# Expert stage of a float32 decoder layer: token tiles of 128 slots instead of 112, and the last 48 slots multiplied by two float32 products side by side, for two steps at once

## The reference

```python
logits = xf @ router_w.T; probs = softmax(logits)
topw, topi = top_k(probs, 2);  topw = topw / (topw.sum(-1) + 1e-06)
...                                       # the 560 heaviest tokens of each expert are kept
disp = zeros(E, capacity + 1, D).at[se, pos].set(xf[st])[:, :capacity]
g = einsum('ecd,edf->ecf', disp, wg)
u = einsum('ecd,edf->ecf', disp, wu)
eo = einsum('ecf,efd->ecd', silu(g) * u, wd)
out = zeros_like(xf).at[st].add(gathered_eo * weight)
```

## Time and profile before

| what | value |
|---|---|
| median of 3 runs | 3836.18 us |
| the profiled execution | 3833.68 us |
| its span in the trace | 3831.9 us |
| PE busy | 3662.7 us (96%) |
| PE weight load | 3157.1 us (82%) |
| DVE busy | 2361.7 us (62%) |
| ACT busy | 1737.3 us (45%) |
| POOL busy | 1298.8 us (34%) |
| granted TensorE clock, mean | 0.979 |

### The profile page before, as it was taken

One profiled execution on the slowest core, in us unless ns is written; L12 is line 12 of the kernel. 1 busy time (PEld: TensorE's weight loads), 2 busy tenths in 40 slices (PEclk: granted clock), 3 DMA queues, 4 the chain that ended last, 5 costly groups with the idle time before them and its releaser, 6 DMA issues. The chain is left out here.

```text
span 3831.9 us, 84885 instructions
## 1 busy us (share of the span) xinstructions
PE 3662.7 (96%) x28086; PEld 3157.1 (82%) x28086; DVE 2361.7 (62%) x5526; ACT 1737.3 (45%) x4277; POOL 1298.8 (34%) x1385
## 2 busy tenths in 40 slices
PE   7999999999979999999999999669999999999998
PEld 6888888888768888888888888459989899899987
DVE  6788888888746666666666666665443433434343
ACT  4555555554535555555555555313333333333332
POOL 1333333333325556665656666310101101011010
PEclk9999999999989999999999999779999999999999
DMA  4222222222343444443444443222433424334232
GB/s 125 59 53 62 53 64 54 61 58 59 89 111 97 106 107 111 109 118 101 108 106 107 112 109 100 61 68 79 115 90 107 115 80 119 87 107 119 82 100 62
DMA packets 315533, 347.68 MB, mean 91 GB/s; under 512 B 45247, under 2 KB 231975, under 8 KB 315396
## 3 DMA queue, kind: packets, MB, share of 16 engines
q1 hardware_dynamic: 305796, 318.25, 30.7%
q0 software_dynamic: 9600, 27.58, 2.5%
HBM read 181.62 MB, written 38.65 MB: 57 GB/s over the span
## 5 line engine op out<-in xcount | busy, mean ns | idle before, releaser
L1605 DVE TENSOR_REDUCE x_mx<-x_psS 112x1 f32<-112x752 f32 x512 | 479.6, 937 | 385.8 <-PE x_psS L1158 382.4
L2339 DVE TENSOR_TENSOR hid<-e_psU,act_g 128x280 f32<-128x280 f32 x256 | 115.2, 450 | 684.5 <-PE e_psU L34 662.5
L1440 ACT ACTIVATE x_pt<-x_psE 125x448 f32<-125x448 f32 x768 | 389.5, 542 | 226.9 <-PE x_psE L1170 217.6
L1029 POOL TENSOR_TENSOR part<-x_pt 125x448 f32<-125x448 f32 x255 | 292.4, 1147 | 509.9 <-ACT x_pt L1440 500.9
L1985 POOL DMA_INDIRECT out<-ex_y,sidx x40 | 38.1, 952 | 1046.0 <-DVE ex_y L2372 1036.9
L611 POOL TENSOR_TENSOR qks<-qks,cos 128x448 f32<-128x448 f32 x128 | 148.1, 1157 | 676.2 <-DMA qks<-qk 676.2
L2130 ACT ACTIVATE act_g<-e_psG 128x280 f32<-128x280 f32 x256 | 103.7, 405 | 470.2 <-PE e_psG L34 456.1
L1158 PE MATMUL x_psS<-k_st,q_st 97*112 97x376 f32 x1024 | 287.7, 362 | 22.8 <-DMA k_st<-mk 14.7
L32 PE MATMUL pj<-xT_hi,win_hi 128*128 128x224 f32 x1024 | 302.7, 296 | 1.5 <-DVE xT_lo L651 1.3
L32 PE MATMUL e_psG<-ex_hi,g_hi 128*128 128x280 f32 x1024 | 303.1, 296 | 0.9 <-issue 0.9
L32 PE MATMUL e_psU<-ex_hi,u_hi 128*128 128x280 f32 x1024 | 298.3, 291 | 3.7 <-DVE hid L2339 2.8
(11 more groups left out here) (293 smaller groups left out, 10712.5 us busy)
## 6 DMA issues: line engine op xcount, KB each, us to landing
k_st<-kT SPq DMA_DIRECT2D x768, 93.8 KB, 2.2
raw_g<-in_L_ffn_wg SPq DMA_DIRECT2D x128, 256.0 KB
raw_u<-in_L_ffn_wu SPq DMA_DIRECT2D x128, 256.0 KB
raw_d<-in_L_ffn_wd SPq DMA_DIRECT2D x128, 256.0 KB
qks<-qk SPq DMA_DIRECT2D x512, 56.0 KB, 2.0
q_st<-qT SPq DMA_DIRECT2D x384, 56.0 KB, 2.0
ctxt<-in_ctx SPq DMA_DIRECT2D x16, 1125.0 KB
xt<-in_x SPq DMA_DIRECT2D x16, 448.0 KB, 3.7
```

The lines of the kernel that those rows point to most:

```text
L1029: pool.tensor_tensor(part[:], pt[j][:, 0, :], pt[j][:, 1, :], ALU.add).then_inc(parted, 1)
L1440: act.activation(pt[j][:, i, :], psE[(j + i) % 2][0:KR, 0:2 * T], ACT.Exp, scale=XD ** -0.5).then_inc(exp_done, 1)
L1605: dve.tensor_reduce(mx[:, j, h:h + 1], psS[0:HT, :, 0:376], AX.XY, ALU.max).then_inc(s_taken, 1)
L2339: dve.tensor_tensor(h[i][:, halves[s]], psU[:, 0:CH], act_g[i][:, halves[s]], ALU.mult).then_inc(S["mul"], 1)
```

## The change

- The 560 slots become 4 tiles of 128 and one of 48 (`SLOTS`, `REST`). The first four go through `mm3` as before, with all 128 partitions in use. Turning and gathering go by tiles of 128 rows.
- The last tile is multiplied only in every other step (and in the closing part), for two steps at once, and in plain float32 straight from `h` and `raw_d`, with no high and low parts: for each of the two steps two products of 48 slots by 256 columns, the left half of D into partitions 0 to 47 and the right half into partitions 64 to 111 of psY[4]. So `split_h` leaves the last 48 slots out.
- The tiles of `down` are dealt anew: in odd steps 0, 1 and 2, 3; in even steps 4, 0 and 1, 2, 3.
- Since `raw_d` of an even step is read until the float32 products of the next even step, d's loads wait for these (`d_used`), or for `up` of the step before, and SP issues them behind g and u of two steps later.
- The last tile's rows of the output are gathered and scattered as half rows (`sides`, `rows_now`), with row numbers of their own, which `tables` makes with some more small instructions. `one_low` compares 16 x 128 numbers.

On TensorE an even step in the middle of an expert looked like this before. The names are destination and sources; e_psY0 to e_psY4 are the banks of the tiles, the digit of d_hi and hid_hi is the parity of the step.

The core of the diff:

```diff
-SLOT_TILES = CAP // HT
+SLOT_TILES = -(-CAP // P)
+REST = CAP - (SLOT_TILES - 1) * P
+SLOTS = [P] * (SLOT_TILES - 1) + [REST]
+HALF_D, HALF_P = D // 2, P // 2
...
-        onelo = [sb(f"onelo{i}", [HT, B, HT], BF16) for i in range(2)]
+        onelo = [sb(f"onelo{i}", [HT, B, P], BF16) for i in range(2)]
...
         halves = (slice(0, CH), slice(CH, CAP))
+        split = (slice(0, CH), slice(CH, CAP - REST))
...
+        sides = out.rearrange("n (h c) -> (n h) c", h=2)
+        def rows_now(t):
+            if t < SLOT_TILES - 1:
+                return out, t, slice(0, D), N - 1
+            return sides, SLOT_TILES, slice(0, HALF_D), 2 * N - 1
...
+                def fetch_down(e, f, i, first, half=None):
...
                     if not first:
-                        hold(sp, S["gate"], S["d_lo"], n - 1)
+                        if i:
+                            hold(sp, S["gate"], S["up"], 4 * (FT * e + f) - 1)
+                        else:
+                            hold(sp, S["gate"], S["d_used"], FT // 2 * e + (f // 2 if isinstance(f, int) else half))
...
+                def fetch_expert(e, start, last):
+                    with sp.Fori(start, FT // 2 - 1) as q:
+                        for i in range(2):
+                            fetch_up(e, 2 * q + 2 + i, i, False)
+                            fetch_down(e, 2 * q + i, i, False, q)
...
-                        m = pe.transpose(psT[:, k * HT:(k + 1) * HT], xg[:, t, k * P:(k + 1) * P], ident[0:HT, 0:HT])
+                        m = pe.transpose(bank[:, k * P:(k + 1) * P], xg[:, t, k * P:(k + 1) * P], ident[:])
...
-                        cols = slice(t * HT, (t + 1) * HT)
-                        m = mm3(pe, psY[t][0:HT, :], (h_hi[i][:, cols], h_lo[i][:, cols]), (d_hi[i][:], d_lo[i][:]), first, last)
+                        cols = slice(t * P, t * P + SLOTS[t])
+                        if t < SLOT_TILES - 1:
+                            m = mm3(pe, psY[t][:], (h_hi[i][:, cols], h_lo[i][:, cols]), (d_hi[i][:], d_lo[i][:]), first, last)
+                        else:
+                            for k in range(2):
+                                for side in range(2):
+                                    m = pe.matmul(psY[t][side * HALF_P:side * HALF_P + REST, 0:HALF_D], h[k][:, cols],
+                                                  raw_d[k][:, side * HALF_D:(side + 1) * HALF_D], start=begins and k == 0,
+                                                  stop=last and k == 1)
+                                if k == 0:
+                                    m.then_inc(S["d_used"], 1)
...
-                        down(m - 1, 1 - i, f == 1, False, 0, 2, None if start else e)
+                        down(m - 1, 1 - i, f == 1, False, (0, 1) if i else (SLOT_TILES - 1, 0), None if start else e, True, f == 2)
...
-                        down(m - 1, 1 - i, f == 1, False, 2, SLOT_TILES)
+                        down(m - 1, 1 - i, f == 1, False, (2, 3) if i else (1, 2, 3), None, False)
...
-                    down(n + FT - 1, 1, False, True, 0, SLOT_TILES)
+                    down(n + FT - 1, 1, False, True, range(SLOT_TILES))
...
+                    for q in range(0, REST, 32):
+                        n = min(32, REST - q)
+                        m = dve.tensor_copy(tok[HALF_P + q:HALF_P + q + n, rows, rest], tok[q:q + n, rows, rest])
+                    done(m)
```

More of the change, by code:

```diff
@@ L1880, in experts @@
         load = {m: [sem(f"load_{m}{i}") for i in range(2)] for m in "gud"}
-        names = ("gate", "gu_hi", "gu_lo", "d_hi", "d_lo", "up", "silu", "mul", "h_hi", "h_lo", "down", "y_full", "y_out",
+        names = ("gate", "gu_hi", "gu_lo", "d_hi", "d_lo", "up", "silu", "mul", "h_hi", "h_lo", "d_used", "y_full", "y_out",
                  "x_up", "x_hi", "x_lo", "wcol", "gidx", "xg", "cur", "scat", "sidx")
@@ L1923, in fetch @@
                     v = w_d[e, cols, :] if isinstance(e, int) else w_d[bass.ds(e, 1), cols, :].rearrange("o p d -> (o p) d")
                     sp.dma_start(raw_d[i][:], v).then_inc(load["d"][i], 16)
+                def fetch_expert(e, start, last):
[3 more added lines that the diff above has]
+                            fetch_down(e, 2 * q + i, i, False, q)
+                    for i in range(2):
+                        if not last:
+                            fetch_up(e + 1, i, i, False)
+                        fetch_down(e, FT - 2 + i, i, False)
@@ L1935, in _ @@
[L1935 to L1938, removed]
+                for i in range(2):
+                    fetch_up(0, 2 + i, i, False)
+                fetch_expert(0, 1, False)
+                with sp.Fori(1, E - 1) as e:
+                    fetch_expert(e, 0, False)
+                fetch_expert(E - 1, 0, True)
                 sp.wait_ge(S["scat"], 16 * SLOT_TILES * E)
@@ L2022, in table, with turn_tile @@
                     m.then_inc(one_used, 1)
+                def turn_tile(t, bank):
+                    for k in range(KD):
+                        m = pe.transpose(bank[:, k * P:(k + 1) * P], xg[:, t, k * P:(k + 1) * P], ident[:])
+                    return m
                 def turn_first():
@@ L2059, in up, with down @@
                     unit(n, i, j, u_hi[i], u_lo[i], psU, s)
[L2061 to L2062 removed]
+                def down(n, i, first, last, tiles, e=None, opens=True, begins=False):
+                    if opens:
                         pe.wait_ge(S["d_lo"], n + 1)
                         pe.wait_ge(S["h_lo"], 2 * n + 2)
[L2065 to L2066 removed]
+                    for t in tiles:
+                        if (begins if t == SLOT_TILES - 1 else first) and e is not None:
                             pe.wait_ge(S["y_out"], SLOT_TILES * e)
[L2068 to L2069 removed]
+                        cols = slice(t * P, t * P + SLOTS[t])
[9 more added lines that the diff above has]
+                                    m.then_inc(S["d_used"], 1)
                         if last:
                             m.then_inc(S["y_full"], 1)
[L2072 to L2073 removed]
                 for i in range(2):
@@ L2133, in split_h @@
                         act.wait_ge(S["mul"], 2 * n + s + 1)
-                        act.activation(h_hi[i][:, halves[s]], h[i][:, halves[s]], ACT.Copy).then_inc(S["h_hi"], 1)
+                        act.activation(h_hi[i][:, split[s]], h[i][:, split[s]], ACT.Copy).then_inc(S["h_hi"], 1)
                     v = 16 * (half + 1 + i)
```

97 lines of the change are left out of this document (51 added, 46 removed).

## The result

| | kernel before | changed kernel |
|---|---|---|
| median, 8 runs each | 3831.97 us (3828.02 to 3836.4) | 3822.06 us (3819.14 to 3827.64) |
| the profiled execution | 3833.68 us | 3824.65 us |
| its span | 3831.9 us | 3822.9 us |
| PE busy | 3662.7 us | 3649.8 us |
| granted TensorE clock, mean | 0.979 | 0.978 |

The ratio is 0.9973, with a 95% interval from 0.9964 to 0.9982: 9.9 us faster. That is just inside the 0.3% that I had called no change, and the time lies in the range; but the forecast was 3831.2 us, so 7.5 us of the gain (against the median) were not foreseen. The traces are taken first, term by term, and then the runs on what they leave open.

A forecast was written before the change was run, and what follows sets the result against it. PE was taken to bound the kernel, busy throughout a mid-expert step; -12.5 + 5.2 + 2.0 + 1.6 + 0.9 + 0.35 = -2.4 us on 3833.68 gave 3831.2 us, range 3818 to 3846.

The forecast's parts named there:

- The group, -12.5: Last 48 slots' down products: float32 group costs 1.19 us per pair of steps, replacing 1.386, 64 times: -12.5 us.
- the fixed 0.33: Float32 group: 0.33 us on top of its streaming, for going into and out of the split array.
- products in turn: Float32 group: its eight records stream one after another, -12.5 becomes +42.5, 3886 us; chance 0.04.
- a load of d that lands late: Even steps: d's load lands more than 7.4 us after issue; 8.4 us would give 3890 us; chance 0.04.
- rival (2): Float32 group: left and right don't pair up; five slots 3845 us or all in turn 3886 us; chance 0.11.
- The closings, +5.2: Where an expert closes: PE's stall for d_lo grows by 0.65 us, 8 times: +5.2 us.
- The turnings, +2.0: Tile turnings of 128 for 112 columns: 0.05 us more each, 35 in the loop plus five first ones: +2.0 us.
- The tables, +1.6: Table products: loading 128 for 112 columns costs 1/7 more, 14 halves at 0.11 us: +1.6 us, at least 0.
- rival (1): Float32 group: the switch is hidden, 3810 us (3820 with half); quick table loads another 5.6 less; chance 0.13.
- The start, +0.9: Before the first expert: two one_low 0.58 us and gathers of 128 rows 0.35 more: +0.9 us (0.6 to 1.5).
- The end, +0.35: At the end: POOL's five scatters in a row take 0 to 0.7 us more: +0.35 us.
- the main case: Whole kernel: the terms as summed hold, 3826 to 3836 us; chance 0.72.

The follow-up runs named there:

- left_then_right: The changed kernel with a group's four float32 products ordered left, left, right, right instead of left and right in turn: 3828.94 us, ratio 0.9970 to the kernel before.
- wide_tables: The kernel before with one_low comparing 128 places for 112, so each table product loads 128 bfloat16 columns: 3827.72 us, ratio 0.9983 to the kernel before.
- padded: The changed kernel with eight unread 4-column products just ahead of TensorE's loop over pairs of experts: 3816.67 us, ratio 0.9949 to the kernel before.
- all_unrolled: The changed kernel with the loops over pairs of experts of TensorE, ScalarE and VectorE written out: 3804.73 us, ratio 0.9932 to the kernel before.
- before_unrolled: The kernel before with the loops over pairs of experts of TensorE, ScalarE and VectorE written out: 3836.40 us, ratio 0.9991 to the kernel before.
- closing_covered: The changed kernel with tiles re-dealt and the float32 group first at closings; a slip makes its output wrong: 3812.32 us, ratio 0.9930 to the kernel before.
- after_again: The changed kernel run once more with no edit: 3827.06 us, ratio 0.9969 to the kernel before.

## Why the prediction was right or wrong

- **The group, -12.5: right.** 64 x 0.19 = 12.2. The streamed 0.86 and the fixed 0.33 both held, and the rivals with products in turn or a load of d that lands late did not come. The fixed part fits the Trainium skill (TensorEngine Tiling, Tiling Modes (Key Properties)), by which a change of the tiling mode drains the array; the page gives no size, and that the mode and not the format makes the 0.33 us is not shown. The span of a packed group in the Trainium skill (TensorE: Matmul & The Clock Gate, Part 3) leaves the 0.33 us out. That the order of left and right matters, on which rival (2) rested, is refuted by left_then_right.
- **The closings, +5.2: right** (+5.1). **The turnings, +2.0: right** (35 x 0.04 = 1.4 and the first ones).
- **The tables, +1.6: wrong in sign**, -5.3 (14 x 0.38), shown by wide_tables alone. The step that failed was to scale the load of 112 columns by 1/7, with "at least 0 if the load is not the bound" as its lower end, and "no row gives a gain". The row it leaned on holds no price of a load: the 0.05 us of the earlier trace rows is the streaming of 224 columns in four strips (0.188/4, as the prediction has it itself), and it is float32. The Trainium skill's rule that I had given beside it (TensorE: Matmul & The Clock Gate, section Weight-path perf modes; its least of about 25 ns stands in that page's Part 1) was right; the estimate of 5.6 us less is what came. It was part of rival (1), and of that only this part came true.
- **The start, +0.9:** from the first one_low to the first up 18.10 us for 18.44, since the first two tables, at 0.59 us for 1.66, paid for it.
- **The end, +0.35: wrong**, -8.6 measured, by leaving out what follows the last scatter. I had looked at the scatters and not at the 12 us between the last of them and the end of the span.
- **Left out: TensorE's jump.** Experts 3 and 5 became 4.5 and 2.9 us longer, where the terms above make them 0.7 shorter each: +8.8. Shown by padded and all_unrolled.
- **Left out: the first step of an expert.** Before, PE waits there for hid in experts 1, 2, 4 and 6 (0.77 to 0.84 us each, by starts less the pace of 0.13), stands on issue in expert 7 (0.99), and has neither in the changed kernel. This is most of the 0.9 us by which an ordinary expert gained more than forecast. But wide_tables does not have this wait either (156.74 us), with the same VectorE code as before, and before_unrolled waits there for act_g. So it changes from one program or execution to the next, and what sets it stays open.

The sum of what was measured, with 5 x 0.9 for the last point: -12.2 + 5.1 + 1.4 - 5.3 - 0.3 - 8.6 + 8.8 - 4.5 = -15.6; the traces have -16.9 from the first one_low on, so 1.3 us are not placed. Against it, the stages ahead of the experts, which the change does not touch, were through 7.9 us later in this profiled execution; -16.9 and +7.9 make the -9.0 between the two spans. Over all profiles that moment lies between 2520.65 and 2529.61 us, at 2520.75 to 2525.74 in the four of kernels with tiles of 112 and at 2520.65 to 2529.61 in the ten others, so an effect of the program of a few us can't be excluded; it stays open.

The time stayed in the range, but 3822.06 us lies outside the 3826 to 3836 that the main case had by its own terms, though its group, its closings and its turnings came as it had them. That it was no further off is in good part luck: two things that I had not seen, -8.6 and +8.8, cancel.

## What to carry to other kernels

Read the stretch behind the last piece of work, and compare the same part of a loop's body where the loop jumps and where it doesn't: each was nearly as large here as the whole measured gain. A change that shifts code can win or lose several us at a far jump (8.8 lost here, most of it won back by eight useless products) without any instruction being slower; before judging such a change, time both kernels with the outer loops written out, or the changed one with a little padding. And the fixed price of going from rounded products to a plain float32 group on half the array and back (0.33 us here) is paid per group, so collect such products.

## What the runs showed of the hardware

- A taken jump of TensorE back over two experts takes 3.3 to 3.7 us before and after (up to 4.2 in closing_covered), and instructions come by DMA in pieces of 16 KB; up to 5.8 us on issue followed (after_again), where PE's first product had to wait for the second piece. The jump of the inner loop over steps takes 0.08 to 0.22 us.
- After such a hole TensorE ran at the 1.2 GHz level for 5.5 us at the changed kernel's first jump and 3.4 at its second (0.23 us between products that otherwise start every 0.13).
- A bfloat16 product of 10 columns with 128 loaded columns starts every 0.026 us, with 112 every 0.05.
- Products in two halves of the array overlap in both orders tried within a group of four; with left, left, right, right the first right one starts 14 ns behind the first left one.
- GpSimd's last drain took 9.86 us in all four profiles of kernels with gathers of 112 rows and 1.28 us in all ten with 128.
